# Moving ten outputs of a recurrent layer into the cross attention that follows it

## The reference

```python
x = x + _L1_attn_ref(_layernorm(x), ...)            # recurrent, below
x = x + _L1_xattn_ref(_layernorm(x), ctx_768, ...)  # cross attention, 16 heads of 16, 154 keys
x = x + _L1_ffn_ref(_layernorm(x), ...)             # mixture of experts
...
i = _bitlinear(hidden_states, w_i, nw_i)
f = sigmoid(_bitlinear(hidden_states, w_f, nw_f))
g = _bitlinear(hidden_states, w_g, nw_g)
h = f * h + (1.0 - f) * i                            # scan over the 1024 rows
o = _rmsnorm(o, g_norm_w) * g * sigmoid(g)
return _bitlinear(o, w_o, nw_o)
```

## Time and profile before

| | us |
|---|---|
| median of 3 runs | 1432.91 (1425.46 to 1433.2) |
| the profiled execution's own time | 1432.4 |
| its span in the trace | 1430.7 |
| recurrent block of the second layer | 808 to 917 |
| cross attention of the second layer | 917 to 1077 |

### The profile page before, as it was taken

One profiled execution on the slowest core, in us unless ns is written; L12 is line 12 of the kernel. 1 busy time (PEld: TensorE's weight loads), 2 busy tenths in 40 slices (PEclk: granted clock), 3 DMA queues, 4 the chain that ended last, 5 costly groups with the idle time before them and its releaser, 6 DMA issues. The chain is left out here.

```text
span 1430.7 us, 27678 instructions
## 1 busy us (share of the span) xinstructions
PE 1296.7 (91%) x9691; PEld 1037.2 (72%) x9691; DVE 1010.1 (71%) x2014; ACT 882.9 (62%) x2215; POOL 457.0 (32%) x628
## 2 busy tenths in 40 slices
PE   4979999999699999989999866689988699999997
PEld 3534444436599999977888654578877699999995
DVE  4687878734566665556788687578875688888773
ACT  4427666774476666645121467478873688888883
POOL 5311222218444333326000356311100244444430
PEclk8979999999899999999999987599998799999998
DMA  4655422200000000003000210022203577777755
GB/s 91 189 122 138 68 46 47 47 1 5 30 2 2 1 2 1 2 6 121 1 0 1 75 24 1 23 62 47 51 10 107 187 232 232 232 233 233 230 158 188
DMA packets 97916, 116.15 MB, mean 81 GB/s; under 512 B 23549, under 2 KB 83187, under 8 KB 97779
## 3 DMA queue, kind: packets, MB, share of 16 engines
q1 hardware_dynamic: 88323, 99.83, 25.7%
q0 software_dynamic: 4416, 12.06, 2.6%
q10 hardware_dynamic: 5040, 2.49, 0.7%
HBM read 88.47 MB, written 16.55 MB: 73 GB/s over the span
## 5 line engine op out<-in xcount | busy, mean ns | idle before, releaser
L827 ACT ACTIVATE sa_probs<-ps 128x512 f32<-128x512 f32 (+1 forms) x304 | 154.5, 577 | 87.6 <-PE ps L780 86.4
L851 DVE TENSOR_REDUCE sa_top<-ps 128x2 f32<-128x1024 f32 (+3 forms) x160 | 171.8, 1114 | 40.9 <-PE ps L756 25.5
L2738 PE MATMUL ps<-me_h,me_w_parts 128*128 128x256 f32 x1104 | 140.9, 288 | 4.8 <-issue 2.9
L2738 PEld LDWEIGHTS ps<-me_h,me_w_parts 128*128 128x128 f32 x1104 | 137.3, 193 | 6.4 <-issue 3.1
L2752 PE MATMUL ps<-me_w_parts,me_mid 128*128 128x256 f32 x1104 | 136.3, 283 | 0.0
L2752 PEld LDWEIGHTS ps<-me_w_parts,me_mid 128*128 128x128 f32 x1104 | 132.4, 188 | 0.0
L3246 ACT ACTIVATE room<-ps,cx_top 128x154 f32<-128x154 f32 x256 | 96.6, 391 | 35.4 <-DVE cx_top L3295 34.9
L2819 DVE TENSOR_TENSOR me_w_parts<-me_chunk,me_w_parts 128x1024 fp32r<-128x1024 f32 x92 | 110.4, 1222 | 9.9 <-ACT me_w_parts L2779 8.3
L2803 ACT ACTIVATE me_full<-ps,me_b 128x256 f32<-128x256 f32 x184 | 95.2, 518 | 34.7 <-PE ps L2738 34.5
L2849 DVE TENSOR_TENSOR me_mid<-me_full,me_mid 128x256 fp32r<-128x256 f32 x184 | 89.9, 506 | 34.7 <-ACT me_mid L2805 34.6
L3125 POOL TENSOR_TENSOR room<-room 128x512 f32<-128x512 f32 x64 | 67.1, 1049 | 140.7 <-DVE room L3303 140.6
(11 more groups left out here) (466 smaller groups left out, 3370.5 us busy)
## 6 DMA issues: line engine op xcount, KB each, us to landing
...
sa_q<-scr_q SPq DMA_DIRECT2D x96, 64.0 KB, 4.7
cn_qd<-cn_qh SPq DMA_DIRECT2D x60, 64.0 KB, 2.0
...
```

The source lines that it names most:

```text
L827: act.activation(probs[:, step % self.PROBS, h0:h0 + many, 0:w], src[:, :, 0:w], ACT.Exp, scale=DH ** -0.5).then_inc(exped.sem, 1)
L851: dve.tensor_reduce(top2[:, k % 2, k0 // 512, h0:h0 + many, sb % HBLK], src[:, :, 0:w], AX.X, ALU.max).then_inc(freed.sem, 1)
L2738: last = pe.matmul(ps[:, MID + n % 4, 0:RT], w[:, u % 2, 0, i, DM * k + P * b:DM * k + P * b + P], h[:, u % 2, j, k, :], start=(m == 0), s ...
```

## The change

The recurrent block gets 19 steps and three more of tail, and makes outputs 0 to 5 only. The queries of pair 0 stand in its steps 15 to 17, and those of pair 1 in steps 18 to 20. Outputs 6 to 15 go into the attention, two to a window: window g (1 to 5) holds tiles 2g+4 and 2g+5, behind `low_q` of pair g. A window's items are `o_round` on POOL, `o_turn` and `o_product` on TensorE, `o_evict` on ScalarE and `o_add` on VectorE with both statistics; its turns and products use the PSUM bank that the queries use. So `turn_x` of pair g+1 waits for window g's last `o_add`. The inverse deviations of those tiles come from `o_var` on VectorE and `o_rstd` on POOL, an integer guess and four Newton steps in 17 chained operations, and the tiles' normals on VectorE wait for them. The scalings of Wq and Wo move from steps 15 to 17 into steps 2 to 4; w_o and a constant are copied ahead of step 0; the rows of the last two tiles are prepared in steps 9 and 10; `front.constants` on POOL goes from tile 3 to tile 11.

The core of the diff:

```diff
-    ROW_STEPS, LAG = (1, 2, 4, 5, 7, 8, 10, 11), 13
-    STEPS = NT + LAG
+    ROW_STEPS, LAG = (1, 2, 4, 5, 7, 8, 9, 10), 13
+    STEPS = NT + 3
+    EARLY = STEPS - LAG
...
+                pool.tensor_copy(nx.w_o[:, :, :], wt[:, 3, :, :]).then_inc(s["kept"].sem, 1)
+                pool.tensor_copy(nx.magic[:, :], magic[:, :]).then_inc(s["kept"].sem, 1)
+                for k in range(STEPS + nx.TAIL):
...
-                    if k + 3 >= LAG and k + 3 < STEPS:
+                    if 0 <= k + 3 - LAG < EARLY:
                         o = k + 3 - LAG
...
-                    if k >= LAG:
+                    if LAG <= k < STEPS:
...
+    TAIL = 3
+    KEPT = NT - 10
+    WINDOWS = {g: range(2 * g + 4, 2 * g + 6) for g in range(1, 6)}
+    PARTS = tuple((t, t + 2) for t in range(6, NT, 2))
 
...
-        if k == 15:
+        if k == 2:
             self.wait(pool, "q_in", 16)
             pool.tensor_scalar(self.wq[:, :, :], self.wq[:, :, :], DH ** -0.5, None, ALU.mult).then_inc(s["scaled"].sem, 1)
-        if k == 16:
+        if k == 3:
...
-        if k == 17:
+        if k == 4:
             self.wait(pool, "q_high", 1)
             pool.tensor_tensor(self.wql[:, :, :], self.wq[:, :, :], raw(self.wqh[:, :, :]), ALU.subtract
                                ).then_inc(s["q_low"].sem, 1)
-        if k in (19, 20):
-            self.wait(pool, "inverted", 1)
-            for t in (2 * k - 38, 2 * k - 37):
-                pool.tensor_scalar(self.xn[:, t, :], c.x[:, t, :], c.rowstat.mv[:, t, 0:1], self.rstd[:, t:t + 1],
-                                   ALU.subtract, ALU.mult).then_inc(s["xn"].sem, 1)
 
...
-        if k == 21:
-            self.turn_x(pe, 0)
-        if k in (22, 23):
-            self.queries(pe, 0, k - 22)
+        if k in (16, 19):
+            self.turn_x(pe, (k - 16) // 3)
+        if k in (17, 20):
+            for m in range(KD):
+                self.queries(pe, (k - 17) // 3, m)
 
     def turn_x(self, pe, g):
         s = self.s
         self.wait(pe, "xn", PAIR * g + PAIR)
         if g:
             self.wait(pe, "ql", g)
+        if g - 1 in self.WINDOWS:
+            self.wait(pe, "o_add", self.WINDOWS[g - 1][-1] + 1 - self.KEPT)
...
+        if k in (15, 18):
+            a = slice(0, 2) if k == 15 else slice(2, 6)
+            self.wait(act, "shifted", 1 if k == 15 else 2)
+            act.activation(self.sd[:, a], self.ve[:, a], ACT.Sqrt).then_inc(s["rooted"].sem, 1)
+        if k in (16, 19):
+            self.high_x(act, (k - 16) // 3)
+        if k in (17, 20):
+            self.high_q(act, (k - 17) // 3)
         if k == 18:
-            self.wait(act, "shifted", 1)
-            act.activation(self.sd[:, 0:4], self.ve[:, 0:4], ACT.Sqrt).then_inc(s["rooted"].sem, 1)
-        if k == 21:
-            self.high_x(act, 0)
-        if k == 23:
-            self.high_q(act, 0)
-        if k == 24:
             self.query_copies(act, 0, 2)
 
...
-        if k == 18:
-            dve.wait_ge(self.c.rowstat.averaged.sem, self.c.rowstat.averaged.at(4))
-            dve.tensor_scalar(self.ve[:, 0:4], mv[:, 0:4, 1], EPS, None, ALU.add).then_inc(s["shifted"].sem, 1)
-        if k == 19:
-            self.wait(dve, "rooted", 1)
-            dve.reciprocal(self.rstd[:, 0:4], self.sd[:, 0:4]).then_inc(s["inverted"].sem, 1)
-        if k == 22:
-            self.low_x(dve, 0)
-        if k == 24:
-            self.low_q(dve, 0)
+        if k in (15, 18):
+            a = slice(0, 2) if k == 15 else slice(2, 6)
+            dve.wait_ge(self.c.rowstat.averaged.sem, self.c.rowstat.averaged.at(a.stop))
+            dve.tensor_scalar(self.ve[:, a], mv[:, a, 1], EPS, None, ALU.add).then_inc(s["shifted"].sem, 1)
+        if k in (16, 19):
+            self.low_x(dve, (k - 16) // 3)
+        if k in (17, 20):
+            self.low_q(dve, (k - 17) // 3)
+
+    def vector_first(self, dve, k):
+
+        if k in (16, 19):
+            i, a = (k - 16) // 3, slice(0, 2) if k == 16 else slice(2, 6)
+            self.wait(dve, "rooted", i + 1)
+            dve.reciprocal(self.rstd[:, a], self.sd[:, a]).then_inc(self.s["inverted"].sem, 1)
+            self.wait(dve, "inverted", i + 1)
+            self.normal(dve, a.start)
+            self.normal(dve, a.start + 1)
+
+    def normal(self, dve, t):
+        dve.tensor_scalar(self.xn[:, t % 4, :], self.c.x[:, t, :], self.c.rowstat.mv[:, t, 0:1], self.rstd[:, t:t + 1],
+                          ALU.subtract, ALU.mult).then_inc(self.s["xn"].sem, 1)
+
+    def o_round(self, pool, o):
+        pool.tensor_scalar(self.zo[:, o, :], self.zo[:, o, :], self.times_o[:, o:o + 1], ROUND, ALU.mult, ALU.add
+                           ).then_inc(self.s["o_round"].sem, 1)
+
+    def o_turn(self, pe, o):
+        n = o - self.KEPT
+        self.wait(pe, "o_round", n + 1)
+        for g, tiles in self.WINDOWS.items():
+            if o == tiles[0]:
+                self.wait(pe, "ql", g + 1)
+        if n:
+            self.wait(pe, "o_add", n)
+        for d in range(KD):
+            last = pe.transpose(self.c.ps[:, self.Q_BANK, P * d:P * d + P], self.zo[:, o, P * d:P * d + P], self.c.ident[:, :])
+        last.then_inc(self.s["o_turn"].sem, 1)
+
+    def o_evict(self, act, o):
+        n = o - self.KEPT
+        self.wait(act, "o_turn", n + 1)
+        act.activation(self.qt[:, :], self.c.ps[:, self.Q_BANK, 0:D], ACT.Identity, bias=self.magic[:, 1:2]
+                       ).then_inc(self.s["o_evict"].sem, 1)
+
+    def o_product(self, pe, o):
+        self.wait(pe, "o_evict", o - self.KEPT + 1)
+        for d in range(KD):
+            last = pe.matmul(self.c.ps[:, self.Q_BANK, D:2 * D], self.qt[:, P * d:P * d + P], self.w_o[:, d, :],
+                             start=(d == 0), stop=(d == KD - 1))
+        last.then_inc(self.s["o_product"].sem, 1)
+
+    def o_add(self, dve, o):
+        n, s, x = o - self.KEPT, self.s, self.c.x[:, o, :]
+        self.wait(dve, "o_product", n + 1)
+        dve.scalar_tensor_tensor(x, self.c.ps[:, self.Q_BANK, D:2 * D], self.unit_o[:, o:o + 1], x, ALU.mult, ALU.add
+                                 ).then_inc(s["o_add"].sem, 1)
+        self.wait(dve, "o_add", n + 1)
+        if n >= 2:
+            self.wait(dve, "o_mean", n - 1)
+        dve.bn_stats(self.o_stats[:, n % 2, :], x).then_inc(s["o_seen"].sem, 1)
+        self.wait(dve, "o_seen", n + 1)
+        dve.bn_aggr(self.c.rowstat.mv[:, o, :], self.o_stats[:, n % 2, :]).then_inc(s["o_mean"].sem, 1)
+
+    def o_var(self, dve, i):
+        a, s = slice(*self.PARTS[i]), self.s
+        self.wait(dve, "o_mean", self.PARTS[i][1] - self.KEPT)
+        dve.tensor_scalar(self.ve[:, a], self.c.rowstat.mv[:, a, 1], EPS, None, ALU.add).then_inc(s["o_var"].sem, 1)
+        self.wait(dve, "o_var", i + 1)
+        dve.tensor_scalar(self.half[:, a], self.ve[:, a].bitcast(I32), 1, None, ALU.arith_shift_right).then_inc(s["o_half"].sem, 1)
+
+    def o_rstd(self, pool, i):
+
+        a, s, link = slice(*self.PARTS[i]), self.s, self.o_link
+        v, y, w = self.ve[:, a], self.guess[:, a], self.work[:, a]
+
+        def then(instruction):
+            instruction.then_inc(link.sem, 1)
+            pool.wait_ge(link.sem, link.next())
+        self.wait(pool, "o_half", i + 1)
+        then(pool.tensor_scalar(y.bitcast(I32), self.half[:, a], -1.0, float(0x5f3759df), ALU.mult, ALU.add))
+        for n in range(4):
+            then(pool.tensor_tensor(w, y, y, ALU.mult))
+            then(pool.tensor_tensor(w, w, v, ALU.mult))
+            then(pool.tensor_scalar(w, w, -0.5, 1.5, ALU.mult, ALU.add))
+            if n < 3:
+                then(pool.tensor_tensor(y, y, w, ALU.mult))
+        pool.tensor_tensor(self.rstd[:, a], y, w, ALU.mult).then_inc(s["inverted"].sem, 1)
 
...
+            if t == 0:
+                for o in self.WINDOWS[1]:
+                    add(("o_round", o, 0), "POOL", 0.46, [])
+            add(("gather", t, 0), "POOL", 1.0, [("exp", t, ns - 1)] + ([("turn", t - 2, 4)] if t >= 2 else [])
+                + ([("o_round", self.WINDOWS[1][-1], 0)] if t == 0 else [])
+                + ([("o_round", self.WINDOWS[t // 2 + 2][-1], 0)] if t % 2 and t // 2 + 2 in self.WINDOWS else [])
+                + ([("o_rstd", t // 2 - 1, 0)] if t % 2 == 0 and 0 < t // 2 <= len(self.PARTS) else []))
+            if t % 2 == 0:
+                for o in self.WINDOWS.get(t // 2 + 2, ()):
+                    add(("o_round", o, 0), "POOL", 0.46, [("gather", t, 0)])
+            elif t // 2 < len(self.PARTS):
+                add(("o_rstd", t // 2, 0), "POOL", 4.7, [("gather", t, 0), ("o_var", t // 2, 0)])
...
-                add(("normal", t, 0), "DVE", 0.36, [("turn_x", t // 2 - 2, 0)] if t >= 6 else [])
-        for g in range(1, NPAIR):
-            add(("turn_x", g, 0), "PE", 0.42, [("normal", t, 0) for t in (2 * g, 2 * g + 1) if t >= 4]
-                + ([("low_q", g - 1, 0)] if g > 1 else []))
+                add(("normal", t, 0), "DVE", 0.36, ([("turn_x", t // 2 - 2, 0)] if t >= 8 else [])
```

(60 more changed lines are left out.)

51 lines of the change are left out of this document (32 added, 19 removed).

## The result

The changed kernel takes 1456.15 us (median of 4 runs, 1454.25 to 1457.52) against 1433.06 us, ratio 1.0172, interval [1.0149, 1.0195]. It is slower by 1.7%, 23.1 us; the forecast was 1456, 23.6 us above the 1432.4 it starts from. The profiled execution took 1454.25 us, its span is 1452.5.

A forecast was written before the change was run, and what follows sets the result against it. The prediction saw a chain of waits in the recurrent tail and an even flow with three nearly full engines in the attention. Stage terms of +20.8 and +3 for the clock on 1432.4 gave 1456 us, range 1428 to 1472.

The forecast's parts named there:

- The step that carried the sum: Attention: queries evicted behind earlier tiles' exps leave 9.1 us of copies partly uncovered four times; +5.9, +9.7, +10.0, +10.0 us.
- Rival C: Attention: copies stay hidden if high_q ends 9.1 us before earlier work runs out; about 1430 us, chance 0.17.
- by 13 us: Attention of the kernel before: the margin by which the copies-stay-hidden condition was said to hold.
- the +3 for the clock: Attention: TensorE may restart slow after dry spells; +1 us for each of three pairs.
- The block's end: Recurrent block: ends with pair 1's chain at 911.9 instead of 917.14 us, -5.2 us.
- The rows' +0.7: Recurrent block: two row tiles moved into earlier steps delay output 1's statistics by 0.7 us, bounds -1.3 to +1.5.
- tile 8 to 10: Attention: time between these tiles' first reductions grows from 17.35 to 27.4 us, +10.0 us.
- Free inside a dry spell: Attention: the windows' added VectorE work, 2.4 us a window, costs nothing where the attention runs dry.
- B: Attention: half clock in all dry pairs, three times +5.8 us instead of +3; about 1470 us, chance 0.14.
- A: Main forecast: the attention runs dry; 1456 us, own range 1443 to 1468, chance 0.56.
- D: Attention: tile normals on VectorE wait for POOL's late chain, five times 3 us more; about 1470 us, chance 0.06.
- E: Recurrent block ends near 898, 19 us earlier, and the windows are hidden; about 1416 us, chance 0.07.

The follow-up runs named there:

- e1: Changed kernel with only raw's planner handicap kept, so query evictions are no longer held back: 1431.62 us, ratio 1.0015.
- e2: Changed kernel with eight other planner handicaps, query evictions of pairs 2 to 7 back at 29 exps ahead: 1421.15 us, ratio 0.9940.
- e5: Kernel before, no output moved, low_x's planner handicap 2.0 in place of 0.15 so query evictions come late: 1497.34 us, ratio 1.0461.
- e3: Changed kernel with four small extra DMAs ahead of each pair's copies from pair 2 on: 1470.69 us, ratio 1.0288.
- e4: Kernel before with four small extra DMAs ahead of each pair's copies from pair 2 on: 1431.67 us, ratio 1.0013.
- e10: Changed kernel in its own order, with the windows' turns, evictions, products, adds and statistics left out: 1447.48 us.
- e6: Kernel before with only the rows of the last two late tiles moved to steps 9 and 10: 1433.36 us, ratio 1.0022.
- e11: Kernel of e2 with normals of tiles 6 to 15 moved to POOL and last two tiles' rows back in steps 10 and 11: 1420.88 us.

## Why the prediction was right

**The mechanism is shown.** The step that carried the sum, that the evictions of pairs 3 to 6 stand behind the exps of the tiles ahead of them, is what e1, e2 and e5 move, in both directions and in both kernels. The planner shifts other items with it, but e3 and e4 move no item and show the copies on the path only where the eviction is late, and e10 and e5 show the long pairs with no window's work. Rival C (the copies stay hidden) is what e2 makes true: its condition, 9.1 us of lead, was the right one, and its price of 1430 was too high. The "by 13 us" beside it is the lead itself (13.7); 4.6 of it is spare, still enough to hide e4's 2.5.

**The terms.** That the total fell on 1456 is in part luck: stages missed by -2.2, +1.5, -0.5, +1.1, +1.9, +2.3 and +1.0 us, the +3 for the clock is inside three of them, and the scatter outside the two blocks took 4.2 off. The block's end came 2.2 us lower than said; its steps held in order: pair 0's queries, output 5 and the scales, then pair 1's chain, which ended it. What I had wrong is the copies on ScalarE's queue, which I had put ahead of pair 1's turn and split. ScalarE's timeline of the kernel after:

```profile
898.07 2.66 ACTq L3456 DMA_DIRECT2D cn_qd<-cn_qh  x4
900.78 0.60 ACT L3619 ACTIVATE cn_xh<-ps 128x512 fp32r<-128x512 f32 x1 [2.51 <-PE ps L3553]
```

They were issued beside the normals and pair 1's turn, and the high part waited for TensorE about as long as for them: the turn ended at 900.43, the last issue at 900.73. The row at 887.49 that the chain starts from is output 0's mean, which the kernel before takes right behind output 1's statistics; the changed kernel takes a tile's mean in the step of its statistics, so output 1's mean stands at that place after, and the start held. The rows' +0.7 is some 1 alone (e6), but in the changed kernel that place came only 0.2 us later (79.46 us into the block against 79.30), and with the rows back in their old steps (e11) at 79.03. The three longest pairs were 1.1 to 2.3 us longer each than their sums. In tile 8 to 10 the exps were 0.8 late and the eviction another 0.2; the copies' 9.1 held; and I had left out the 0.8 us from the first score at 1022.49 to the reduction at 1023.28. The sum of +35.0 for three pairs against 29.7 exceeds the +3 put down for the clock by 2.3.

**Where a step failed.** "Free inside a dry spell" is wrong: e10 gives 8.7 us for the windows in the dry order, 4.7 of it in the four dry pairs by the traces. A likely reason, not shown by itself, is that a window's product and add stand in the same chain as the leftovers, since turn_x waits for them; e10 takes out that wait with the work. And I had forecast some 4 us of idle TensorE before each dry pair; 7.5 us in four were measured, as the leftovers filled more of the copies' 9.1.

**The rivals.** B (half clock throughout): the clock does fall to 0.50 at the start of the pairs of tiles 8 and 10, but stands at 0.86 and 0.84 over them (994 to 1023, 1023 to 1053 us), and the time is A's. The Trainium skill ("TensorE: Matmul & The Clock Gate", section "HAM oscillation — how this bites in real kernels") says of a matmul kernel with DMA waits between its batches that every batch starts slow. The trace agrees for those two pairs, and not for tile 6's, which begins at 1.00 (965 to 970 us) behind a wait of 1.12 us. D (POOL's chain late): in the profile after no wait of VectorE for POOL is listed in 905 to 1100 us, and POOL itself sat idle before the chain:

```profile
996.67 0.19 POOL L3716 TENSOR_SCALAR cn_guess<-cn_half 128x2 int32<-128x2 int32 x1 [13.81 <-DVE cn_half L3705]
996.95 0.19 POOL L3718 TENSOR_TENSOR cn_work<-cn_guess 128x2 f32<-128x2 f32 x1
```

Its 17 operations are 0.28 us apart, 4.7 in all (5.1 predicted). E (the tail really goes) did not come: pair 1's chain ended the block, as said against it, since its normals at 898.52 came behind output 5's mean at 895.85 and the scales.
